# First attention: GpSimd's subtraction as a tensor-by-scalar instruction, and twelve root tiles and four log tiles instead of eleven and five

## The reference, cut to what matters

```python
q, k = _l2norm(to_heads(q)), _l2norm(to_heads(k))          # 16 heads, head size 8, 2048 tokens
cos = jnp.einsum('bhsd,bhtd->bhst', q, k)
g_dist = jnp.arccos(jnp.clip(cos, -1.0 + EPS, 1.0 - EPS))
attn_score = (1.0 + g_dist) ** (-3.2)
n_r = jnp.sum(attn_score, axis=-1)
n_c = jnp.sum(attn_score, axis=-2)
k_tilde = attn_score / n_r[..., :, None] / n_c[..., None, :]
probs = k_tilde / jnp.maximum(jnp.sum(k_tilde, axis=-1, keepdims=True), 1e-12)
out = jnp.einsum('bhst,bhtd->bhsd', probs, v)
```

## Time and profile before

| | us |
|---|---|
| median of 3 runs | 3676.81 |
| lowest and highest | 3673.8, 3677.45 |
| profiled execution, device time | 3673.4 |
| its span, first to last instruction | 3671.6 |
| mean granted TensorE clock, share of full speed | 0.831 |

### The profile page before, as it was taken

The page is one execution under the profiler, slowest core; times in us unless marked ns, Lnnn a source line. Parts: engine busy times, 40 slices in busy tenths (PEclk is TensorE's granted clock), DMA queues, the critical chain, the costliest instruction groups (busy, mean ns, idle before and its releaser), DMA issues. The chain is left out here.

```text
span 3671.6 us, 59781 instructions
## 1 busy us (share of the span) xinstructions
PE 3125.7 (85%) x19264; PEld 1305.2 (36%) x19264; DVE 2831.9 (77%) x4045; ACT 3014.8 (82%) x2658; POOL 2666.5 (73%) x1450
## 2 busy tenths in 40 slices
PE   4888888898888988889886758888888888888899
PEld 2322222222122221222213323555555555555547
DVE  7678988888888888888887977877878778788301
ACT  1799999999999999999995645887878888788822
POOL 2698988989889898898882424776767777677600
PEclk8776677766777667776677977999999999999999
DMA  0100000000000000000001450010000110000100
GB/s 23 53 7 7 1 6 7 6 7 2 4 7 6 7 4 3 7 6 6 5 5 38 139 161 24 25 47 25 24 25 24 34 38 24 25 24 25 39 0 12
DMA packets 59508, 85.46 MB, mean 23 GB/s; under 512 B 9808, under 2 KB 45904, under 8 KB 58960
## 3 DMA queue, kind: packets, MB, share of 16 engines
q1 hardware_dynamic: 59344, 83.06, 7.9%
HBM read 52.44 MB, written 30.54 MB: 23 GB/s over the span
## 5 line engine op out<-in xcount | busy, mean ns | idle before, releaser
L1177 POOL TENSOR_TENSOR lo<-pr,hi 128x1024 f16<-128x1024 f32 x384 | 917.3, 2412 | 383.8 <-ACT hi L1303 381.7
L1226 DVE TENSOR_REDUCE mx<-mx_ps 128x1 f32<-128x512 f32 x1024 | 660.0, 684 | 164.8 <-PE mx_ps L1341 161.5
L1318 ACT ACTIVATE pr<-s_ps 128x1024 f32<-128x1024 f32 x512 | 531.8, 1039 | 264.3 <-PE s_ps L1362 234.7
L1303 ACT ACTIVATE hi<-pr 128x1024 f16<-128x1024 f32 x512 | 548.1, 1071 | 0.0
L1341 PE MATMUL mx_ps<-ka,qa 128*128 128x512 f16 x1024 | 386.1, 398 | 142.4 <-DVE mx L1226 117.3
L671 ACT ACTIVATE wt<-wt 128x2048 f32<-128x2048 f32 x256 | 485.0, 1895 | 0.5
L477 POOL TENSOR_TENSOR wt<-base,wt 128x1024 f32<-128x1024 f32 x192 | 459.9, 2395 | 15.1
L662 ACT ACTIVATE wt<-wt,theta_bias 128x10240 f32<-128x10240 f32 (+2 forms) x96 | 464.3, 4837 | 0.8
L1381 PE MATMUL pv_ps<-vh,hi 128*128 128x129 f16 x4096 | 432.0, 222 | 11.6 <-ACT sums L1309 5.3
L1360 PE MATMUL s_ps<-qa,ka 128*128 128x512 f16 x1024 | 395.9, 387 | 35.2 <-issue 22.4
L473 POOL TENSOR_TENSOR base<-base,shift 128x1024 f32<-128x1024 f32 x192 | 363.7, 1894 | 84.6 <-DVE base L527 84.6
(11 more groups left out here) (197 smaller groups left out, 5292.7 us busy)
## 6 DMA issues: line engine op xcount, KB each, us to landing
qk<-stg SPq DMA_DIRECT2D x6, 2048.0 KB, 13.4
vh<-v SPq DMA_DIRECT2D x16, 520.0 KB, 3.5
qa<-qk SPq DMA_DIRECT2D x16, 512.0 KB, 3.3
ka<-qk SPq DMA_DIRECT2D x32, 256.0 KB, 4.8
v<-v_st SPq DMA_DIRECT2D x3, 2080.0 KB, 7.9
qst<-parts_dram SPq DMA_DIRECT2D x144, 32.0 KB
kst<-parts_dram SPq DMA_DIRECT2D x144, 32.0 KB
qk<-stg SPq DMA_DIRECT2D x4, 1024.0 KB, 8.7
```

What stands on the lines that cost most here:

```text
L1177: eng.tensor_tensor(lo[:, i % NHL, :, :], pr_slot(i), hi[:, i % NHL, :, :], ALU.subtract).then_inc(lo_done, 1)
L1226: eng.tensor_reduce(mx4[:, q // NCH, q % NCH:q % NCH + 1], mx_ps[:, q % 2, :], AX.X, ALU.max)\
L1303: eng.activation(hi[:, i % NHL, :, :], pr_slot(i), ACT.Copy).then_inc(hi_done, 1)
L1318: eng.activation(pr_slot(i), s_ps[:, i % 2, :, :], ACT.Exp, scale=SM).then_inc(exp_done, 1)
```

## The change

`NL` becomes 4, so `NQ` becomes 12: root tiles 0 to 11, log tiles 12 to 15, `PAIRS` (two, two), `GROUPS` (0, 4, 8, 11, 14, 15, 16). The fourth group now holds root tiles 7, 8 and 9, and NQ - 3 is 9. POOL's subtraction of a broadcast column becomes a tensor-by-scalar instruction with two operations, an addition of the negative constant and a multiplication by 1. The column `shift` and its memset are gone. Since the number of wide chunks no longer fits the rotation of three slots, the first four wide chunks (folding tile 4 and the first log tile) rotate over the two halves of `m_ps`, and three slots are used from the fifth on. One planner constant changes.

```diff
-NL = 5
+NL = 4
...
-    assert (RS - R1) % 3 == 2
+    TWO = R1 + 2 * ((2 - RS + R1) % 3)
...
-    ROOT_US, CHUNK_US, PRODUCT_US, LOAD_US, LAG_US = 0.954, 0.625, 4.35, 1.3, 2.0
+    ROOT_US, CHUNK_US, PRODUCT_US, LOAD_US, LAG_US = 0.954, 0.625, 3.75, 1.3, 2.0
...
-        theta_bias, shift = t("theta_bias", [P, 1]), t("shift", [P, 1])
+        theta_bias = t("theta_bias", [P, 1])
...
-            q = (r - R1) % 3 if r < RS else (r - R1 + 2) % 3
+            q = (r - R1) % 2 if r < TWO else (r - TWO) % 3 if r < RS else (r - TWO + 2) % 3
...
-                        eng.tensor_tensor(v, v, shift[:, 0:1].to_broadcast([P, 2 * BANK]), ALU.subtract)\
-                           .then_inc(shifted, 1)
+                        eng.tensor_scalar(v, v, -K2 * G4 * G4, 1.0, ALU.add, ALU.mult).then_inc(shifted, 1)
...
-                eng.memset(shift[:, :], K2 * G4 * G4)
...
-                        free = R1 if r == R1 + 2 else r - 2 if r <= RS + 1 else r - 4 if r < RS + 3 else RS + 1
+                        free = r - 1 if r < TWO + 2 else R1 if r == TWO + 2 else r - 2 if r <= RS + 1 else r - 4 if r < RS + 3 else RS + 1
```

## The result

| | before | after |
|---|---|---|
| median, us | 3675.31 (4 runs) | 3821.97 (4 runs, 3810.34 to 3826.13) |
| ratio to before | 1 | 1.0395 (95%: 1.0369 to 1.042) |
| profiled execution, us | 3673.4 | 3819.02 |
| its span, us | 3671.6 | 3817.1 |
| granted TensorE clock | 0.831 | 0.816 |

The kernel after is 4% slower, although its busiest engine in the first attention has 46.7 us less to do. The forecast was 3794 us. The measured median lies inside the stated range of 3765 to 3845, but above 3815, where the forecast's own range ended; the rest of the range was there for a slow POOL instruction.

A forecast was written before the change was run, and what follows sets the result against it. Two equally long loops bound it: ACT alone, and sigmoid, DVE's wide phase and ACT's tail. Per inner head 4.1 + 3.6 - 0.2 = 7.5 us, together +117.5, gave 3794 us; own range 3770 to 3815, stated range 3765 to 3845.

The forecast's parts named there:

- The bound: First attention: ACT alone and the loop of sigmoid, DVE's wide phase and ACT's tail equally long, within 0.3 us.
- One log tile fewer on ACT: ACT loses one sigmoid and one arc tangent, 3.6 us a head, of which only 1.4 us is gained.
- DVE's wide phase: DVE drops two log halves (-2.26 us), adds one root tile (+6.80), and loses a 0.83 us wait for POOL.
- Two slots: Four wide chunks on two slots instead of three delay DVE by 0.4 us, bounds 0 and 1.0.
- ACT's tail: From the fourth logarithm on, a longer logarithm (+1.7) and one more score (+1.9): +3.6 us, less up to 0.2.
- ACT's wait ahead of it: ACT idle before the fourth logarithm, waiting for DVE's closing pass: over 5 us, 4 to 6 as a sign.
- the rival with ACT alone: ACT's own work stays the bound, so the kernel gets faster: 3654 or 3619 us; chance 6%.
- POOL: POOL's new subtraction takes 1.3 us, between 1.05 and 2.39; off the path below 1.63 us.
- the 2.39 case: POOL's new subtraction as slow as its two-input product: at least +11 us a head, over 3850 us.
- Only the last logarithm binds: The fourth logarithm does not wait; only the closing of the last root tile counts: +3.2 us a head, 3728; chance 5%.
- POOL's new instruction is no faster: Above 1.63 us POOL joins the path: 3837 us at 1.89, over 3850 at 2.39; chance 9%.
- the three signs of being wrong: DVE's wide pace under 1.1 us, no ACT idle before the fourth logarithm, DVE waiting for POOL over 1 us a head.

The follow-up runs named there:

- experiments 6 and 9: 6: kernel after with single-tile late logarithms, smaller first sigmoids, earlier last PE chunks, 3723.52 us; 9: that plus earlier rows, values and spread weighings, 3706.83 us.
- the second experiment: Kernel before with only POOL's subtraction exchanged for the tensor-by-scalar form: 3676.08 us against 3676.86, ratio 0.9998.
- the seventh experiment: Kernel before's five log tiles with the new subtraction, sigmoids of 1, 2 and 2 tiles, single logarithms for the last four root tiles: 3690.17 us, ratio 1.0039.

## Why the prediction was right, and where it was off

*The bound.* Right. The Trainium skill (Perfetto Trace Analysis, section Identifying the Most-Contended Engine) would have ACT, the engine of highest occupancy, optimized first; here 46.7 us of its busy time went and the kernel became 147 us slower. What decided was that two loops were equally long before, ACT's own work and the chain through DVE. That the chain is what grew is shown by the split of the group, an experiment, and not by the trace alone.

*One log tile fewer on ACT.* Right in kind: ACT waits for DVE ahead of both arc tangents (1.35 and 1.20 us) and cannot use the 3.6 us. It is through with them 537.73 - 484.43 = 53.3 us after the head's start, where it was at 53.96, so 0.7 us are gained and not 1.4; the difference is the later start below.

*DVE's wide phase.* Right: the pace stays 6.79 us a tile with POOL's new instruction, so the faster instruction did not speed DVE up, and the 0.83 us wait is gone.

*Two slots.* Right in size: the eight log halves take 534.00 - 524.56 = 9.44 us, 0.39 over 8 x 1.131, forecast 0.4. It is split as forecast too: the fifth half starts 529.18 - 524.56 = 4.62 us behind the first, 0.1 over 4 x 1.131, and 0.3 come behind it, where DVE waits 0.21 us for PE.

*Start of the chain.* This is the term that was missing. I took the 39.4 us from head start to log tiles as given; it became 524.56 - 484.43 = 40.1, since ACT's root and log halves end 35.1 to 35.5 us after the start where they ended at 34.33. That adds 0.8 to 1.2 us a head. With it, the closing of tile 9 is 4.75 us later and not 4.1. The sum had nothing for it; the own range had half a microsecond a head for PE at another clock, which is too little.

*ACT's tail.* 20.58 us against 17.18: +3.40, forecast 3.4. Period of the fourth head: 4.75 + 3.40 - 0.13 (the short wait before the fourth logarithm that was there already) = +8.02.

*ACT's wait ahead of it.* This reading was wrong. I expected ACT idle "over 5 us", and 4 to 6 as a sign of being right; measured are 7.20 us there and 1.47 ahead of the third logarithm, 8.67 in all. The prediction's own terms give it: the closing 4.1 later, ACT 1.4 earlier through its arc tangents, and the 1.7 and 1.9 us that have moved behind the wait, together 9.1 less the 0.2 us by which the pass was already early. The last two were counted in the tail and forgotten here. The time does not depend on it, since the tail starts from DVE's pass. The condition of the rival with ACT alone has the same slip: for ACT to be 1.4 us earlier at the head's end, `closed(9)` would have to end some 5 us before today's 562.6 and not 1.4, since 3.6 us more work follow it.

*POOL.* Its price was 1.3 us in the prediction and 1.047 measured, at my lower bound of 1.05 from the casts. Both are below the point of 1.63 us, so that changes nothing, and the price of the old form with twelve tiles, +2.7 a head, came out at 2.83. (The rest of POOL's busy time in the 2.39 case is 103.97 - 22 x 4.289 = 9.6 us and not 9.8; nothing hangs on it.)

*The sum.* Forecast 117.5 us, measured 145.5 in span. Heads: (122.79 - 114.81) x 16 = 128. The other 17 us come from stages that the change does not touch, 12.3 of them from the second attention, and the prediction put these at nothing (next section but one). Both misses have the same sign. The mechanism was right, and the size fell short by 28 us. That the median of 3822 us is still inside the stated range is luck: its upper end of 3845 stood for a slow POOL instruction, which did not come, and the own range ended at 3815.

*The rivals.* "Only the last logarithm binds" was priced at 3728 us. The split group brought 3733, but by other meetings, tiles 8 and 10. The rival with ACT alone is out: ACT stood idle 13.3 us a head, and even with the chain shortened (experiments 6 and 9) its 3.6 us did not come through. "POOL's new instruction is no faster" is out with 1.047 us.

*The signs.* Seen as named: heads 122.79 us apart, 20.58 us from the fourth logarithm to the load, POOL waiting more, and none of the three signs of being wrong. Close or missed: ACT busy 109.2 us a head ("near 108.5"), 2.55 us of waits ahead of the arc tangents ("1"), and the wait of 7.20 us above ("4 to 6").

## What to carry to other kernels

Before work is taken off the busiest engine, find for each of its instructions what it would meet if it came earlier. Where a producer already finishes just in time, moving work to that producer costs its whole duration, plus whatever work the move puts behind the wait (here 4.1 and 3.6 us a head as forecast). A grouped instruction waits for the last of its members: put the cut where the producer is late, so that members ready earlier are not held back (here one more instruction a head was followed by 89 us less). And price a form of instruction by a row of exactly that form. A sum of terms can be right while a wait read off beside it is not: add up the idle time of an engine (period less busy time) and see whether the waits named account for it. Here the prediction's 121.8 less 108.5 gave 13.3 us, 11 more than before, and the new waits it named came to 5 to 7.

## What was not expected of the hardware

**The tensor-by-scalar instruction on GpSimd.** 128x1024 in f32 took 1.047 us with two operations, 2.770 with one, and the broadcast subtraction 1.894. The Trainium skill (GPSIMD Engine Reference, section 3.1) sets two-input instructions at about 2.6 cycles an element and bodies with k up to 2, which I read as one input and up to two operations, at 1.03; at its 1.2 GHz that is an estimate of 0.88 us for 1024 columns. The trace is near it for the form with two operations: the casts of the earlier trace rows give 0.82 ns a column and, worked out from their two sizes, 0.21 us that do not grow with the columns; the sum is an estimate of 1.05 us. For the form with one operation the trace is far from it. Why one operation is slower was not tried; that kernel had one run, in which all 384 such instructions took 2.77 to 2.78 us.

**TensorE's clock at a head's start.** In the first 35 us of a head the granted clock was 0.99 to 1.00 in the kernel before (from the third head on). In the kernel after it was 0.95 or 0.96 in the first five heads and 0.90 in the other eleven. The fourth head of each:

```profile
465.50:500.50 35.00, 30.42 (x132) 9.21 (x125) 27.92 (x47) 33.36 (x35) 29.90 (x16) 0.99 0.00 0
```

```profile
484.40:519.50 35.10, 28.98 (x110) 9.02 (x110) 27.86 (x47) 33.12 (x35) 25.46 (x16) 0.95 0.00 0
```

PE in the next head of the kernel after:

```profile
609.29 0.61 PE L717 MATMUL m_ps<-mst 109*128 109x512 f16 x2 [2.64 <-ACT wt L641]
...
611.95 0.63 PE L748 MATMUL r_ps<-mst 110*128 110x512 f16 x1
612.38 1.06 PE L717 MATMUL m_ps<-mst 109*128 109x512 f16 x2
...
614.95 0.59 PE L717 MATMUL m_ps<-mst 109*128 109x512 f16 x2
```

Two 512-column matmuls take 0.61 us at 609.29, 1.06 at 612.38 and 0.59 at 614.95: the upper of the two levels (2.4 GHz), then the lower (1.2 GHz) for about 4 us, then the upper again. Ahead of it PE had stood idle for 2.64 us, waiting for ACT to begin the new head. In the sixth kernel, with weighings up to the head's start, the clock was 1.00 from 582 to 590 us.

The cost shows best inside one kernel. In the second experiment, from the third head on, ACT is through with its root and log halves after 34.33 us in every head but the ninth. There it takes 35.41 us, the head is 1.08 us longer (115.36 against 114.28), and the clock is 0.95. The eighth head and the ninth:

```profile
922.90:957.90 35.00, 29.66 (x126) 9.07 (x119) 27.94 (x48) 33.36 (x35) 26.44 (x16) 1.00 0.00 0
1037.10:1072.10 35.00, 29.52 (x114) 9.03 (x110) 28.03 (x47) 32.49 (x35) 25.73 (x16) 0.95 0.00 0
```

PE's idle time ahead of the squares was 2.12 us in that ninth head and at most 1.78 in the others from the third on. But in the seventh experiment heads with 1.2 and 1.3 us of it had the lower clock too. So a dip of the clock goes with about 1 us a head, and the idle time just ahead of it does not decide alone when it comes; it was not varied by itself.

**Unchanged stages took longer.** The second attention, the same instructions in all kernels, took 1206.0 us in the kernel before (2184.7 to 3390.7), 1213.7 and 1208.6 in the two others with five log tiles, and 1218.3 in the kernel after, 1211.5 to 1225.2 in the seven others with four. The two groups overlap, each number is from one execution, and runs of one kernel lie up to 16 us apart, so that the number of log tiles matters here is not shown. The busy times of DVE, ACT and POOL in it are equal within 1 us between the kernels before and after; PE's are 1045.7 and 1051.8.

```profile
2184.70:3390.70 1206.00, 1045.68 (x10462) 634.31 (x10463) 958.93 (x1344) 945.78 (x1007) 849.04 (x355) 0.96 0.10 28
```

The granted clock is 0.96 here and 0.95 in the kernel after. Whether the clock is the cause, and whether it depends at all on a stage that is over, is open.
